# Causal masking in a two-layer transformer kernel: zeroed exponentials on GpSimd in place of mask matmuls on TensorE

## What is computed

```python
q, k, v = heads(x @ Wq + bq), heads(x @ Wk + bk), heads(x @ Wv + bv)   # 16 heads of 16 channels
att = einsum('bhqd,bhkd->bhqk', q, k) * scale
att = where(tril(ones((T, T))), att, -inf)                             # T = 512
y = einsum('bhqk,bhkd->bhqd', softmax(att, axis=-1), v)
y = y + (the same with keys and values of the context, not causal)
```

## Time and profile before

| | |
|---|---|
| time, median of 3 runs | 1824.35 us (1822.88 to 1830.0) |
| the profiled execution, its own time | 1824.27 us |
| its span, first to last instruction | 1822.5 us |
| mean granted TensorE clock | 0.953 |
| PE matmuls busy | 1643.0 us, 90% |
| DVE busy | 1356.4 us, 74% |
| ACT busy | 1151.3 us, 63% |
| POOL busy | 663.0 us, 36% |

### The profile page before, as it was taken

How to read it: one execution, slowest core, us unless ns; L and a number is a source line. 1 busy time by engine, 2 the same in 40 slices (tenths; PEclk the granted TensorE clock), 3 DMA queues, 4 the chain that set the end, 5 groups by cost and what they waited for, 6 DMA issues and landing times.

```text
span 1822.5 us, 29171 instructions
## 1 busy us (share of the span) xinstructions
PE 1643.0 (90%) x10064; PEld 735.4 (40%) x10064; DVE 1356.4 (74%) x2549; ACT 1151.3 (63%) x2178; POOL 663.0 (36%) x915
## 2 busy tenths in 40 slices
PE   5898799998999999998999899998999988899677
PEld 1344345433543345433543344333544443333236
DVE  6667867788687877777777868877487687687287
ACT  1474585666665686667655675657655854765497
POOL 3435323551454134532454135523561242310140
PEclk7899999999999999999999999999999997999899
DMA  7444313323142323332242324233232231123123
GB/s 193 127 113 123 81 36 100 88 82 88 55 116 71 94 66 102 88 103 59 81 107 77 87 60 111 73 103 87 77 105 51 61 98 44 44 83 133 47 70 117
DMA packets 106947, 159.49 MB, mean 88 GB/s; under 512 B 20656, under 2 KB 83248, under 8 KB 106800
## 3 DMA queue, kind: packets, MB, share of 16 engines
q1 hardware_dynamic: 101904, 156.43, 30.8%
q10 hardware_dynamic: 4896, 1.18, 0.3%
HBM read 105.00 MB, written 51.38 MB: 86 GB/s over the span
## 4 chain that ended last, share of the span: by engine, by line
PE 57%; DVE 19%; ACT 11%; POOL 6%; issue 4%; DMA 2%; SPq 1%; ACTq 0%; DVEq 0%; POOLq 0%
PE acc L1495 12%; PE st L1481 11%; PE misc L1460 11%; DVE nmax L1258 8%; PE misc L1435 7%; PE misc L1407 4%; PE misc L1522 3%; ACT probs L991 3%; PE misc L1447 3%; ACT tail_h L1061 2%; ACT tail_h L1046 1%; PE misc L1536 1%; PE misc L1549 1%; PE st L1484 1%; POOL parts L876 1%
## 5 line engine op out<-in xcount | busy, mean ns | idle before, releaser
L1258 DVE TENSOR_REDUCE nmax<-misc 128x1 f32<-128x512 f32 (+2 forms) x1376 | 864.3, 672 | 294.1 <-PE misc L1460 169.3
L991 ACT ACTIVATE probs<-st 128x512 f32<-128x512 f32 (+3 forms) x1536 | 760.1, 551 | 371.8 <-PE st L1481 239.7
L1460 PE MATMUL misc<-stack 96*128 96x512 bf16 (+3 forms) x1536 | 536.1, 365 | 61.5 <-DVE nmax L1258 43.5
L1481 PE MATMUL st<-stack 99*128 99x512 bf16 (+3 forms) x1536 | 542.4, 364 | 36.3 <-ACT probs L991 30.9
L1481 PEld LDWEIGHTS st<-stack 99*128 99x128 bf16 x1536 | 148.9, 98 | 376.7 <-ACT probs L991 219.4
L1460 PEld LDWEIGHTS misc<-stack 96*128 96x128 bf16 x1536 | 152.1, 99 | 203.4 <-DVE nmax L1258 86.9
L870 POOL TENSOR_TENSOR parts<-qk,zero 128x512 bf16<-128x512 f32 x78 | 81.3, 1043 | 224.1 <-ACT qk L974 224.1
L1495 PE MATMUL acc<-probs,v_x 128*32 128x512 f32 x1152 | 159.8, 628 | 0.0
L1495 PE MATMUL acc<-probs,v_s 128*32 128x512 f32 (+3 forms) x1152 | 114.3, 469 | 0.1
L1484 PE MATMUL st<-mask_st,identb 128*128 128x128 bf16 x512 | 111.2, 220 | 0.0
L882 POOL TENSOR_TENSOR nparts<-nmax,zero 128x16 bf16<-128x16 f32 x96 | 22.2, 231 | 242.8 <-DVE nmax L1258 242.8
(11 more groups left out here) (261 smaller groups left out, 2094.5 us busy)
## 6 DMA issues: line engine op xcount, KB each, us to landing
parts_xk<-parts SPq DMA_DIRECT2D x54, 128.0 KB
parts_xq<-parts SPq DMA_DIRECT2D x54, 128.0 KB
stack<-parts_xq SPq DMA_DIRECT2D x36, 192.0 KB, 3.1
stack<-parts_xk SPq DMA_DIRECT2D x36, 192.0 KB, 3.6
parts_sk<-parts SPq DMA_DIRECT2D x48, 128.0 KB
parts_sq<-parts SPq DMA_DIRECT2D x48, 128.0 KB
stack<-parts_sq SPq DMA_DIRECT2D x32, 192.0 KB, 2.9
stack<-parts_sk SPq DMA_DIRECT2D x32, 192.0 KB, 3.4
```

Of the source, the lines that this page charges most:

```text
L991: act.activation(probs[:, j % P_SLOTS, c, T - w:], st_bank(n, 4 * j + c)[:, 0:w], ACT.Exp, scale=SCALE).then_inc(exp_done, 1)
L1258: dve.tensor_reduce(nmax[:, ring, first:first + NT * (len(cs) - 1) + 1:NT], src, AX.X, ALU.max, negate=True).then_inc(misc_free[slot], 1)
L1460: last = pe.matmul(o, stack[0:ROWS, r, 0, c, P * i:P * i + P], stack[0:ROWS, r, 1, c, 0:w], start=True, stop=not causal)
L1481: last = pe.matmul(o[:, 0:w], stack[0:AUG, r, 1, c, P * j:P * j + P], stack[0:AUG, r, 0, c, T - w:T], start=True, stop=not causal)
```

## The change

The mask matmul of the causal scores is left out. Instead POOL sets the exponentials above the diagonal to zero, once for each key tile of an s unit, for all four heads in one `affine_select` on the 128 x 4 x 128 block of `probs`; it does so at the step `scores(j, 3)` of the list. `values` of an s unit waits for that (`probs_masked`) and no longer for the exponentials. `probs` gets a third slot, used in turn over all tiles. v is laid out with 18 columns a head in place of 32; a weight load still takes 32 columns, the last 14 of which now belong to the next head (or to a zeroed rest at the end).

```diff
-ST_BANKS, MISC_BANKS, P_SLOTS, QK_RING = 3, 4, 2, 4
+ST_BANKS, MISC_BANKS, P_SLOTS, QK_RING = 3, 4, 3, 4
+V_STEP = D + 2
...
-        v_aug = {p: lb(f"v_{p}", [P, NT, H, 32]) for p in "xsf"}
+        v_flat = {p: lb(f"v_{p}", [P, NT * H * V_STEP + 32 - V_STEP]) for p in "xsf"}
+        v_aug = {p: v[:, 0:NT * H * V_STEP].rearrange("p (t h e) -> p t h e", t=NT, h=H) for p, v in v_flat.items()}
...
+        def v_columns(s, p, j, h):
+
+            first = (j * H + h) * V_STEP
+            return v_flat[v_name(s, p)][:, first:first + 32]
...
+        def probs_slot(n, j):
+
+            return n.times(NT, j).slot(P_SLOTS)
+
+        def masked_tiles(s, j):
+
+            return (s.unit[0] * NU + s.unit[2]) * NT + j + 1
...
-            for v in v_aug.values():
+            for p, v in v_aug.items():
                 pool.memset(v[:, :, :, D:D + 1], 1.0).then_inc(consts_made, 1)
                 pool.memset(v[:, :, :, D + 1:], 0.0).then_inc(consts_made, 1)
+                pool.memset(v_flat[p][:, NT * H * V_STEP:], 0.0).then_inc(consts_made, 1)
...
+            def scores(s):
+                j, c = s.args
+                if s.unit[1] == "s" and c == HU - 1:
+                    diagonal = probs[:, probs_slot(s.n, j), :, P * j:P * j + P]
+                    pool.wait_ge(exp_done, s.n.times(16, 4 * j + 4 + ST_BANKS).at())
+                    pool.affine_select(out=diagonal, in_=diagonal, compare_op=ALU.is_ge, fill=0.0, base=0,
+                                       pattern=[[0, HU], [1, P]], channel_multiplier=-1).then_inc(probs_masked, 1)
...
-                act.activation(probs[:, j % P_SLOTS, c, T - w:], st_bank(n, 4 * j + c)[:, 0:w], ACT.Exp, scale=SCALE).then_inc(exp_done, 1)
+                act.activation(probs[:, probs_slot(n, j), c, T - w:], st_bank(n, 4 * j + c)[:, 0:w], ACT.Exp, scale=SCALE).then_inc(exp_done, 1)
...
                 last = pe.matmul(o[:, 0:w], stack[0:AUG, r, 1, c, P * j:P * j + P], stack[0:AUG, r, 0, c, T - w:T],
-                                 start=True, stop=not causal)
-                if causal:
-                    last = pe.matmul(o[:, 0:P], identb[:, :], mask_st[:, :], start=False, stop=True)
+                                 start=True, stop=True)
...
-                pe.wait_ge(exp_done, n.times(16, 4 * j + 4 + ST_BANKS).at())
+                if p == "s":
+                    pe.wait_ge(probs_masked, masked_tiles(s, j))
+                else:
+                    pe.wait_ge(exp_done, n.times(16, 4 * j + 4 + ST_BANKS).at())
                 for c in range(HU):
-                    last = pe.matmul(acc[32 * c:32 * c + 32, T - w:T], v_of(s, p)[:, j, HU * g + c, :],
-                                     probs[:, j % P_SLOTS, c, T - w:T], start=j == 0, stop=j == NT - 1)
+                    last = pe.matmul(acc[32 * c:32 * c + 32, T - w:T], v_columns(s, p, j, HU * g + c),
+                                     probs[:, probs_slot(n, j), c, T - w:T], start=j == 0, stop=j == NT - 1)
```

More of the change, by code:

```diff
@@ L462, in two_layers_kernel @@
         ident, identb = sb("ident", [P, P]), sb("identb", [P, P], BF16)
-        mask_st, mask_mx = sb("mask_st", [P, P], BF16), sb("mask_mx", [P, P], BF16)
+        mask_mx = sb("mask_mx", [P, P], BF16)
         minus_half, magic, zero = sb("minus_half", [P, NT]), sb("magic", [P, 1]), sb("zero", [P, 1])
@@ L499, in two_layers_kernel @@
         NFIRST = 6
-        NMADE = 13
+        NMADE = 15
         consts_in, consts_made = sem("consts_in"), sem("consts_made")
@@ L507, in two_layers_kernel @@
         st_full, exp_done = sem("st_full"), sem("exp_done")
-        values_done = sem("values_done")
+        values_done, probs_masked = sem("values_done"), sem("probs_masked")
         heads_full, rsum_done = sem("heads_full"), sem("rsum_done")
@@ L550, in y_of, with v_name @@
             return {("f", B - 2): xn["A"], ("f", B - 1): y["x"]}.get((p, batch(s)), y[p])
+        def v_name(s, p):
+            return {("f", B - 2): "x", ("f", B - 1): "s"}.get((p, batch(s)), p)
         def v_of(s, p):
-            return v_aug[{("f", B - 2): "x", ("f", B - 1): "s"}.get((p, batch(s)), p)]
+            return v_aug[v_name(s, p)]
+        def v_columns(s, p, j, h):
+            first = (j * H + h) * V_STEP
+            return v_flat[v_name(s, p)][:, first:first + 32]
         def parts_of(b, w):
@@ L804, in _ @@
             pool.memset(ones1[:, :], 1.0).then_inc(consts_made, 1)
-            for n, t_ in enumerate((ident, identb, mask_st, mask_mx)):
+            for n, t_ in enumerate((ident, identb, mask_mx)):
                 pool.memset(t_[:, :], 0.0).then_inc(zeroed, 1)
@@ L810, in _ @@
                                    pattern=[[-1, P]], channel_multiplier=1).then_inc(ident_made, 1)
-            pool.wait_ge(zeroed, 4)
-            pool.affine_select(out=mask_st[:, :], in_=mask_st[:, :], compare_op=ALU.is_ge, fill=MASKED, base=0,
-                               pattern=[[1, P]], channel_multiplier=-1).then_inc(consts_made, 1)
+            pool.wait_ge(zeroed, 3)
             pool.affine_select(out=mask_mx[:, :], in_=mask_mx[:, :], compare_op=ALU.is_ge, fill=MASKED, base=0,
                                pattern=[[-1, P]], channel_multiplier=1).then_inc(consts_made, 1)
-            for v in v_aug.values():
+            for p, v in v_aug.items():
                 pool.memset(v[:, :, :, D:D + 1], 1.0).then_inc(consts_made, 1)
                 pool.memset(v[:, :, :, D + 1:], 0.0).then_inc(consts_made, 1)
+                pool.memset(v_flat[p][:, NT * H * V_STEP:], 0.0).then_inc(consts_made, 1)
             pool.memset(xrun[:, :], 0.0).then_inc(consts_made, 1)
@@ L908, in down_q @@
                 pool.tensor_tensor(hq[:, t % 2, :], hid[:, t, :], magic[:, :].to_broadcast([P, F]), ALU.subtract).then_inc(hq_full, 1)
-            walk(pool, dict(consts_rest=consts_rest, stats=stats_, norm=norm, mid_bias=mid_bias, project=project, negmax=negmax,
+            walk(pool, dict(consts_rest=consts_rest, stats=stats_, norm=norm, mid_bias=mid_bias, project=project, negmax=negmax, scores=scores,
                             y_T=y_T, hid_scale=hid_scale, down_q=down_q))
@@ L1474, in scores @@
                 (j, c), n, r = s.args, s.n, s.n.slot(STACKS)
-                causal = s.unit[1] == "s"
-                w = T - P * j if causal else T
+                w = T - P * j if s.unit[1] == "s" else T
                 if (j, c) == (0, 0):
```

## The result

| | before | after |
|---|---|---|
| time, median of 4 runs each, side by side | 1826.35 us (1822.88 to 1830.0) | 1940.59 us (1933.36 to 1944.04) |
| ratio, 95% interval | | 1.0623 [1.0596, 1.0650] |
| span of the profiled execution | 1822.5 us | 1940.1 us |
| mean granted TensorE clock | 0.953 | 0.921 |

The account below looks back on a forecast made before the run. PE was taken to set the time of the s units almost alone; 1824.3 - 30 (masks) + 110 (waits) - 5 (given back) + 20 (clock) = 1919 us, 5% slower, range 1865 to 1972 us.

Parts of the forecast that it names:

- Masks, -30 us: Removing 512 mask matmuls of about 0.059 us each on PE, in s units that PE bounds, gains 30 us.
- The low bound, 23 us: Lower bound of the mask gain, if the s1 units, which DVE bounds, give their 7.5 us back.
- Selects, 0.9 us each: 128 added selects on POOL take 0.9 us each, bounds 0.62 and 1.16 us; 115 us of POOL time.
- Waits, +110 us (96 to 124): PE's values wait for selects queued behind POOL's splits and negmax: 15.3 us a turn in turns 2 to 5, +110 us.
- Given back in s1, -5: In s1 PE already waits and DVE uses a stall to catch up: -5 us, 0 to -12.
- Clock, +20 us: Half-rate PE stretches after some 35 long stalls, 0.6 us each, from 0 to 1.7: +20 us, 0 to 60.
- Contention and later POOL steps, 0 and 0: Selects beside DVE's work: 0 to 20 us, taken as 0; later x and f splits: 0, at most 0.9 us a select.
- Third slot, 18 columns, 0: The third slot for exponentials and values at 18 columns a head cost nothing.
- Repaying stalls (1844 us): Rival, chance 0.08: only the first stall of s0 and of s2-s3 is paid, about 50 us, giving 1844 us.
- Faster (1794): Rival, chance 0.05: selects are ready in time and only the 30 us gain remains; decided at 3.8 us a turn.
- The collapse of the clock (1978): Rival, chance 0.07: every long stall costs its full 1.7 us, 60 us in place of 20, with the upper select.
- What would show it: Signs listed beforehand: values waiting for selects over 90 us in 40 to 60 waits, longer s0, s2, s3, clock below 0.953.

Follow-up runs that it names:

- e5: Changed kernel with matmuls of nothing put ahead of the five long waits of the s units of batches 1 to 5: 1907.4 us, ratio 1.0442.
- e7: Changed kernel with POOL's splits of queries and keys over 128 of 512 values, selects and waits unchanged: 1794.99 us, ratio 0.9827.
- e6: Changed kernel with values one key tile later in the order of every unit, all selects in place: 1841.09 us, ratio 1.0070.
- e4: Changed kernel with selects over one head's block in place of four, all waits kept: 1908.96 us, ratio 1.0448.
- e2: Changed kernel with selects run on a spare block nobody reads; values wait for the exponentials alone: 1848.92 us, ratio 1.0113.
- e3: Kernel before, mask matmuls kept, with only the third slot for exponentials and v at 18 columns a head: 1824.78 us, ratio 0.9990.
- e8: e6 with POOL's sum of heads moved ahead of its bias sum in the list: 1867.75 us, ratio 1.0230.
- e12: e6 with s1 masked by matmuls, not selects; PE's transposes of the sum of heads later in f0, those ahead of it sooner: 1853.33 us.

## Why the prediction was right, and where it was off

1. **Masks, -30 us: -15.** The step that failed is "all on PE in units that PE bounds". In turn 3 it was true for 0.53 to 0.85 us of a unit's 0.94, over all turns for 14.5 us of some 22.5 in s0, s2 and s3. s1 gave 0.5 us of 7.5, in turns 1 to 5 less than nothing, and f0 met POOL's sum, for which PE waited 0.41 us already. The low bound, 23 us, took s0, s2 and s3 in full.
2. **Selects, 0.9 us each: 0.66.** Inside the bounds, near the low one, the growth of a memset. From 128 to 512 values it grew by (661 - 319) / 384 = 0.89 ns a value, where the memsets had 0.87. The Trainium skill (GPSIMD Engine Reference, Performance pitfalls for Q7 kernels) has 1.03 cycles an element for unrolled compare-and-select; at its 1.2 GHz that is 0.86 ns, an estimate from that page, and these runs agree with that and not with the 2.03.
3. **Waits, +110 us (96 to 124): 95.4 in 41 waits, longest 4.8.** Turn 3 tile by tile, forecast and measured: 2.5 and 2.61; 1.6 and 1.27; 2.6 and 2.61; 3.9 and 3.40; 3.4 and 3.41. The two short ones, 0.7 and 0.6, did not come, since PE was at half rate then and itself late: in e5, at full clock, they are there, 0.77 and 0.53. 13.3 us in place of 15.3; that the chain with a select of 0.62 us had given 13.4 is in part luck, as it counts the two short waits. Batches 0, 1, 6 and 7 were put at 15, 15, 12 and 6 and have 15.0, 13.1, 10.4 and 3.0. Laying out POOL's queue by hand gave each of the five long waits to 0.5 us; e7 and e6 show that the queue is the cause.
4. **Given back in s1, -5:** not seen. In turn 3 s1 became 2.1 us longer. But in e4 s1 has a wait of 0.92 us, the clock stays at 1.00, and s1 takes 12.8 us, no longer than before, so that this wait was given back. In after a wait of 1.27 us, the half-rate stretch behind it and a DVE that is busy for 1.0 us longer took it.
5. **Clock, +20 us: about 33** for five of eight batches (e5). The term was mis-sized: 0.6 us a wait, on the ground that POOL's queue drains in a slow stretch and shortens the next wait. It was 1.3 us (0.7 to 2.0), by its middle nearer to the upper end, 1.7: the five long waits came at nearly their full length, and only the two short ones were saved.
6. **Contention and later POOL steps, 0 and 0:** good enough for the sum, wrong as a reason. In the f units, where POOL's sum of heads would be late, after loses nothing on balance (534.1 us against 534.0). But e2 shows that selects on POOL cost 35 us where PE does not wait for them. By the sum below these 35 us are not on top in after. A likely reason, which no run shows, is that POOL and DVE catch up while PE stands at `values`. The contention itself is there: the layer norm's operation on DVE takes 502 ns on average in after, 410 in before, and DVE is busy for 13.47 us in s1 of turn 3 in place of 12.45. "At most the 0.9 us of a select each" was too low as well, 2.0 us in f0, as four selects add up ahead of one sum.
7. **Third slot, 18 columns, 0:** right (e3).

The sum by measured terms: -15 + 95 + 33 = +113 us, against 117.6 us between the two spans. The last term alone is uncertain by 16 us either way, so that the 4 or 5 us that have no term tell nothing; the clock behind the waits of batches 0, 6 and 7, which e5 left unfilled, would belong there. The forecast, -30 + 110 - 5 + 20 = +95, was 22 us short: 15 by the masks, 13 by the clock and 5 by s1, less 15 of waits too many, make 18; the rest has no term, as said. That the masks and the waits were each off by 15 us in opposite directions, and so cancel, is luck.

**The rivals.** Repaying stalls (1844 us) would have left only two waits a turn; there are five. Faster (1794) would have needed at most 3.8 us of waits a turn, there are 13.3; and its price was too good, since even without any wait the kernel stands at 1813. The collapse of the clock (1978) had the right direction: 1.3 us a wait lies between my 0.6 and its 1.7, and the interval of e5 does not exclude the latter.

**What would show it** came as listed: the select as what PE's values wait for, over 90 us in 40 to 60 waits (41, the longest 4.8 us, none in an x or f unit), s0, s2 and s3 longer by 3.1, 3.1 and 8.1 us, the clock below 0.953.

**Open:** how much of e2's and e6's remainder is DVE beside POOL and how much POOL's lateness. The rows separate them only in s1 and f0 of turn 3; no run took the one away without the other.

## What to carry to other kernels

Before a step is moved to an engine with a low busy share, lay it into that engine's queue at its exact place: the price is what stands ahead of it when the consumer asks (here 2.6 us for 0.64 us of work), far more than its own length. A wait on the bounding engine can cost more than its length, here about 1.3 us of slow clock for each of the 25 that e5 filled and nothing for the 0.92 us in s1 of e4, and freeing the bounding engine pays only as far as the next engine is early, here half. In a list that all engines walk, moving one step moves it on each of them, so look at every engine's neighbours of that step first (e8, e12).

## What the runs showed of the hardware beyond what was expected

How little idle time the clock answered to. Windows in s1 of turn 3 of after:

```profile
762.00:764.40 2.40, 0.89 (x10) 0.26 (x10) 2.19 (x7) 1.03 (x4) 1.97 (x4) 1.00 0.58 162
764.40:765.40 1.00, 1.00 (x11) 0.34 (x12) 1.00 (x4) 0.00 (x0) 0.54 (x1) 1.00 1.04 231
765.40:768.80 3.40, 3.40 (x21) 2.42 (x22) 2.32 (x6) 1.97 (x6) 0.00 (x1) 0.55 0.89 207
```

1.51 us of idle time in 2.40 us, its longest piece 1.27 us, were followed by 3.4 us at 0.55, while e6's wait of 1.61 us in f0 left that window at 1.00: the length of one wait alone does not tell it here. Matmuls on a constant, put into the waits, kept the clock at 1.00 from s0 to f0 of turn 3 (e5). DVE's two-input operation over 512 values took 0.69 us alone and 1.53 us beside POOL's split operation and a select; four operations of the layer norm took 1.38 us alone and 2.07 us beside selects. POOL's select fared alike: 0.64 us alone, and beside DVE's split

```profile
751.00 0.85 POOL L912 TENSOR_SCALAR_AFFINE_SELECT probs<-probs 128x512 f32<-128x512 f32 x1 [1.75 <-ACT probs L1016]
```
